# Edge-major one-hots of the two attention passes made on ScalarE in a four-layer graph network kernel

## The reference, cut to what matters

```
for l in range(2):
    xn = layernorm(h);  q, k, v = xn @ wq + bq, xn @ wk + bk, xn @ wv + bv
    scores = einsum('ehd,ehd->eh', q[dst], k[src]) * scale     # 8 heads of 32
    m  = segment_max(scores, dst);  ex = exp(scores - m[dst])
    z  = segment_sum(ex, dst);      attn = ex / z[dst]
    agg = segment_sum(attn[:, :, None] * v[src], dst)
    h = h + agg @ wo + bo;  h = h + gelu(layernorm(h) @ w1 + b1) @ w2 + b2
```

## Time and profile before

| | us |
|---|---|
| median of 3 runs | 6895.34 (6890.48 to 6896.88) |
| profiled execution | 6895.29 |
| span of the profiled execution | 6893.5 |

### The profile page before, as it was taken

The page is one execution under the profiler, slowest core; times in us unless marked ns, Lnnn a source line. Parts: engine busy times, 40 slices in busy tenths (PEclk is TensorE's granted clock), DMA queues, the critical chain, the costliest instruction groups (busy, mean ns, idle before and its releaser), DMA issues. The chain is left out here.

```text
span 6893.5 us, 55872 instructions
## 1 busy us (share of the span) xinstructions
PE 3674.6 (53%) x14811; PEld 2847.0 (41%) x14811; DVE 3431.6 (50%) x6662; ACT 1000.6 (15%) x2079; POOL 3392.8 (49%) x3358
## 2 busy tenths in 40 slices
PE   1373256662001455554666666685666659764542
PEld 1263155551001344443344444674454448333331
DVE  7594344443000444556677777446777762222225
ACT  0000122211000111111211111332111113210000
POOL 4787766668886455550254453004454410037662
PEclk9655567766555577776788887897888879886666
DMA  1142233441100233332455554115555530233333
GB/s 38 28 101 41 46 113 113 117 87 30 18 2 8 82 94 94 94 88 55 148 158 154 155 159 111 42 51 163 151 163 152 154 78 13 104 122 93 93 91 55
DMA packets 289794, 630.52 MB, mean 91 GB/s; under 512 B 79692, under 2 KB 134320, under 8 KB 286384
## 3 DMA queue, kind: packets, MB, share of 16 engines
q0 software_dynamic: 168256, 437.11, 25.6%
q1 hardware_dynamic: 121328, 190.89, 8.6%
HBM read 560.35 MB, written 66.48 MB: 91 GB/s over the span
## 5 line engine op out<-in xcount | busy, mean ns | idle before, releaser
L862 PE MATMUL edge_sums<-edge_rows,edge_hot 128*128 128x272 f32 (+3 forms) x4640 | 1518.4, 491 | 896.2 <-issue 241.3
L809 POOL DMA_INDIRECT edge_rows<-kv_rows,dst_index x928 | 879.8, 948 | 1547.7 <-POOLq L89 668.1
L862 PEld LDWEIGHTS edge_sums<-edge_rows,edge_hot 128*128 128x128 f32 x4640 | 1112.6, 248 | 1207.7 <-issue 411.1
L809 POOL DMA_INDIRECT edge_rows<-rel_rows,dst_other_index x464 | 466.4, 1005 | 755.3 <-ACTq L89 565.2
L1102 PE MATMUL edge_own_rows<-dst_x,edge_hot_t 128*128 x1856 | 615.6, 490 | 163.2 <-DVE edge_rows L936 118.4
L809 POOL DMA_INDIRECT edge_rows<-xl_rows,dst_index x464 | 457.9, 987 | 464.3 <-PE edge_sums L862 249.0
L809 POOL DMA_INDIRECT edge_rows<-rows,src_index x464 | 454.1, 979 | 235.5 <-issue 127.3
L1102 PEld LDWEIGHTS edge_own_rows<-dst_x,edge_hot_t 128*128 128x128 f32 x1856 | 442.6, 248 | 301.0 <-issue 220.5
L211 POOL DMA_INDIRECT table_dst<-proj_dst_put_stage x350 | 418.4, 1195 | 97.8 <-issue 86.2
L1019 DVE TENSOR_TENSOR edge_rows<-edge_rows,edge_turn_p 128x2048 f32<-128x2048 f32 x174 | 396.6, 2280 | 119.1 <-ACT edge_rows L1181 119.0
L872 DVE TENSOR_TENSOR l_acc<-l_acc,edge_sums 128x258 f32 (+1 forms) x464 | 197.9, 427 | 496.0 <-PE edge_sums L862 212.6
(11 more groups left out here) (389 smaller groups left out, 5386.5 us busy)
## 6 DMA issues: line engine op xcount, KB each, us to landing
edge_where<-local_dst SPq DMA_DIRECT2D x174, 256.0 KB
dst_rank_keys<-in_dst SPq DMA_DIRECT2D x85, 312.5 KB
rel_rows<-proj_out SPq DMA_DIRECT2D x25, 1024.0 KB
edge_where<-local_src SPq DMA_DIRECT2D x58, 256.0 KB
edge_rows<-kv_rows,dst_index POOLq DMA_INDIRECT x928
kv_rows<-proj_out SPq DMA_DIRECT2D x50, 260.0 KB, 2.0
edge_rows<-rows,src_index POOLq DMA_INDIRECT x464
edge_rows<-xl_rows,dst_index POOLq DMA_INDIRECT x464
```

Of the source, the lines that this page charges most:

```text
L809: pool.indirect_dma_start(out=self.rows[:, h * U + b, 0:self.width], out_offset=None, in_=self.source[:, :], in_offset=bass.IndirectOffset ...
L862: last = nc.tensor.matmul(sums[p % len(sums)][:, 0:width], self.hot[s % 2][:, 2 * (p % 4) + i, :], self.half(s)[:, 2 * (p % 4) + i, first: ...
```

## The change

In the attention passes DVE no longer calls `mark`. ACT makes the same one-hots in `mark_by_act`: eight Abs instructions, one per tile of 128x128, give |place - column| (the place comes in as the bias of each partition), and, after they are complete, one Relu over 128x1024 gives 1 - that, so 1 where they are equal and 0 elsewhere. ACT calls it for half 2c behind spot(2f+2), ahead of both exponentials, and for half 2c+1 behind `place`, ahead of spot(2f+3). The wait for a free buffer (`summed`) moves from DVE to ACT. The other passes keep DVE's `mark`.

```diff
-        self.hotted = ph.sem("hotted")
+        self.hotted, self.apart = ph.sem("hotted"), ph.sem("apart")
...
+    def mark_by_act(self, nc, act, s, summed):
+
+
+        after(act, summed, 4 * (s - 1))
+        hot = self.hot[s % 2]
+        for t in range(HT):
+            last = nc.scalar.activation(hot[:, t, :], self.k.ramp[:, :], ACT.Abs, scale=-1.0,
+                                        bias=self.order.local[:, s * HT + t:s * HT + t + 1])
+        last.then_inc(self.apart, 1)
+        act.wait_ge(self.apart, s + 1)
+        flat = hot[:, :, :].rearrange("p t e -> p (t e)")
+        nc.scalar.activation(flat, flat, ACT.Relu, scale=-1.0, bias=self.k.ones[:, 0:1]).then_inc(self.hotted, 1)
...
-                if chunk(c):
+                if chunk(c) and not dot:
                     e.mark(nc, dve, 2 * c, summed)
 
                 if chunk(f) and dot:
                     multiply(4 * f + 2)
                 if chunk(c):
                     weigh(2 * c)
-                    e.mark(nc, dve, 2 * c + 1, summed)
+                    if not dot:
+                        e.mark(nc, dve, 2 * c + 1, summed)
...
                 e.spot(nc, act, 2 * f + 2, expanded)
                 if chunk(c):
+                    if dot:
+                        e.mark_by_act(nc, act, 2 * c, summed)
                     act.wait_ge(faced, c + 1)
                     nc.scalar.activation(drop[:, :], drop[:, :], ACT.Exp).then_inc(factored, 1)
                     act.wait_ge(lowered, c + 1)
                     nc.scalar.activation(raised_t[:, :], raised_t[:, :], ACT.Exp).then_inc(raised, 1)
                     place(c)
+                    if dot:
+                        e.mark_by_act(nc, act, 2 * c + 1, summed)
                 e.spot(nc, act, 2 * f + 3, expanded)
```

## The result

| | us |
|---|---|
| before, median of 4 runs | 6894.12 (6890.48 to 6896.88) |
| changed, median of 4 runs | 6812.99 (6806.62 to 6828.34) |
| ratio | 0.9886, interval 0.9874 to 0.9898 |
| profiled execution of the changed kernel | 6806.62, span 6804.7 |

The changed kernel is 81 us faster. The prediction was 6812, range 6757 to 6869. The kernel before took 6877 to 6894 us in two of the comparisons here (called long) and 6404 to 6417 in the three others (called short), steadily within each and with both kinds seen on the same chip, so every kernel is compared only with the runs of before beside it.

What follows compares the result with a forecast made beforehand. DVE's chain of ordered work and hand-overs was taken to bound the attention passes. 6895.29 - 132 (marks) + 35 (late waits at multiply and weigh) + 14 (late adds) = 6812 us, range 6757 to 6869.

Steps and rivals of the forecast that it cites:

- DVE's order is one chain: Attention passes: DVE's work in order plus hand-overs sets the pace; 116 marks of 1.135 us removed give 132 us.
- the nine instructions are hidden: On ACT, per half: eight Abs and one Relu take 2.9 us, bounds 2.1 and 3.7, costing nothing on the path.
- late semaphores of PE keep part of the gain: At DVE's waits for PE and `place`: counts some 5 us late in 35 of 58 steps, late adds too; loss 35 + 14.
- 35 us at multiply(4f+2) and weigh: In 35 late steps DVE, without the first mark, arrives 1.13 us earlier and waits; mean loss 1.0 us, together 35.
- 14 at the adds: Before `add` of pair 7: late semaphores eat up to 1.13 x 24 = 27 us more; half taken, 14.
- The sign given for the first term: On DVE: L1019 gets idle time ended by L1181, and L936 more, some 50 us together.
- signs of being wrong: `form` or L862 waiting on ACT, a step under 28.5 us, or late adds exceeding 24 by more than ten.
- its upper bound: Forecast's own case: whole loss at the add and 20 us more, as contiguous gathers end later against L1192; 6846.
- they hang on gather traffic: PE's late semaphores were tied to gather traffic, as `place` is on time in the last two steps, without gathers.
- all of it arrives: Rival: late semaphores move with DVE's chain or are fewer; 6895 - 132 = 6763, down to 6757 us; chance 0.16.
- Gathers setting the pace: Rival: the gathers set the pace of the passes and nothing arrives, 6895 us; chance 0.07.
- an outcome slower than before: Rival: denser gathers make semaphores late every step at weigh(2c) and add of pair 7; 202 against 132, 6965 us; chance 0.07.

Runs made afterwards that it cites:

- The two kernels with copies: Kernel before and changed kernel, each with one 799 KB DRAM-to-DRAM copy per half in the attention passes: 6885.89 and 6791.77 us, beside 6876.94 for before.

## Why the prediction was right, step by step

- That DVE's order is one chain and a mark counts 1.135 us, 132 in all: right. Where semaphores are on time the change gives 138 us (6404.34 to 6266.36, interval 127 to 145), and the step goes down to 26.6 us. The 6 us over the sum are inside that interval.
- That the nine instructions are hidden: right, with a size off. I took 2.9 us for them and 3.7 as the bound; they take 3.6. The trace has 0.40 us for one Abs and 0.29 from Abs to Abs (2.45 - 0.40 over seven); my 0.2 from the narrow tiles was low. The spacing is the 0.29 that the prediction estimated from the rule of the Trainium skill ("VectorE: DVE Perf Modes", TRN2 errata). Nothing hung on it: double the Abs is level with single.
- That late semaphores of PE keep part of the gain: right as far as the traces can show it. DVE's waits grew by 48 us, about what is missing (next point), and with semaphores on time nothing is missing; no run changed their lateness alone. The mean step of the profiled execution is 29.24 us, forecast 29.2, from 30.63. The two long comparisons give 81 and 94 us, the three short ones 138, 137 (with twice the Abs) and 130 (with cut gathers).
- How the loss is shared between its two terms: wrong, and the total is right by luck. I wrote 35 us at multiply(4f+2) and weigh, 14 at the adds. From the first `fix` on, DVE's idle time before the multiplies rose by 5.2 and 1.9 us in the two passes, before weigh by 1.6 and 3.4, together 12; before the adds by 19.4 and 16.9, together 36. The two kernels with copies repeat it: 17 us and 34. The failed step is the one that held the late steps fixed and moved only DVE: late steps went from 37 to 29 of 58, while the waits moved in among the adds. Per step DVE waited 1.85, 0.50, 1.33 and 1.66 us before pairs 4 to 7 and now waits 2.18, 0.91, 1.95 and 1.00 (first pass): the late one used to fall on pair 7 and now falls on any. That need not be the work of the change: before's kernel with copies, marks and all, has 2.15, 0.72, 1.82 and 0.73. The sum, 48 against 49, came out by two errors that cancel. The sign given for the first term, some 50 us more before L1019 and L936, did not come; of the signs of being wrong none did (no wait of `form` or L862 for ACT, a step of 29.2 us, and 22 waits of 2.35 us or more before the adds of pairs 5 to 7, where there were 25). One sum is off by one: its upper bound adds up to 6845, not 6846.
- That they hang on gather traffic: not shown. They are absent with full gathers in three comparisons, and copies do not add to them. Yet where the time goes speaks for something near it. Laid side by side, PE's instructions in the long and the short run of the changed kernel, the same program, start together until the first of the five passes over the edges. The long run then loses 74, 223, 95, 93 and 41 us in these five passes, the only stretches with gathers of edge rows, and 2 us in all the rest together. These are also the stretches in which the engines hand work to each other in small pieces, and no run tells the two apart. Loading of instructions is no rival: in the first attention pass both runs have 18 such transfers of 16 KB and 24 of 8 KB, and in before's trace none falls into the late step of the earlier trace rows. Nor are the gathers slower: half of their packets take 161 ns or less in both. The cause is open; that the late semaphores belong to the condition of a comparison and not to the kernel or the chip is shown by the one chip that gave both.
- The rivals: "all of it arrives" came true, but in the short comparisons. Gathers setting the pace is ruled out for these by the cut gathers, and an outcome slower than before by every comparison.

## What to carry to other kernels

An engine that is busy for 73% of a stage (683.67 of 931 us here) can still be the chain that sets the pace: count where its idle time stands, and an instruction outside of those places is worth its start-to-start time, wherever else it can be hidden. Before work is moved to another engine, look whether the same time can be had by putting it into the first engine's own waits: here two instructions moved by a few lines gave 145 us on top of the change, about as much as the change itself. When a wait ends with another engine's, at the same instant and far after the work that should release both, treat it as a wait of its own kind: bound what it can eat of a gain, look at more than one trace of the same kernel, and do not take from one trace where it will fall.

## What the runs showed of the hardware that was not expected

- The same kernel on the same chip took 6404 us in one comparison and 6877 in the next, each within 0.3%. With it goes how soon TensorE's semaphores are counted. `place` begins 0.9 us after the exponential in all 58 steps of the short run of the changed kernel, and up to 6.5 us after it in half of them in the long one. In a late step TensorE's own next instructions start all the same (3982.82, above), and four counts come within 0.18 us. All of the longer time, 526 of 528 us, lies in the five passes over the edges.
- Gathers of a thirteenth of the bytes, 27 GB/s against 163 to 168, change nothing in a short comparison (0.9996), and 46 GB/s of further copies in a long one cost 9 us.
- 1905 equal matmuls took 495 us in one kernel and 517 in another that differs only in which of two equal instructions was taken off VectorE, at a granted clock of 0.92 and 0.89. The products of pair 3 follow 2.5 us of idle time of TensorE in the one and 4.5 in the other, and run at a mean granted clock of 0.85 and 0.55.
